# First stage of a two-layer graph network: only the destinations loaded beside x, chunk work moved between the table groups, both zeroings moved behind the first pairs and the first pass

## What is computed

```python
h = jnp.maximum(_layernorm(x), 0.0)
xl, xr = h @ Wl + bl, h @ Wr + br                      # first layer (attention)
m = leaky_relu(xl[src] + xr[dst] + edge_weight1 * We, 0.2)
alpha = softmax of (m @ att) over the edges of one dst
h = gelu(h + segment_sum(alpha * xl[src], dst) + bias)
x = x + batch_norm(h)
h = jnp.maximum(_layernorm(x), 0.0)                    # second layer (messages)
em = relu(layer_norm([h[src], h[dst]] @ msg_w + msg_b)) * edge_weight
messages = mean of em over the edges of one dst
x = x + gate * relu(layer_norm([h, messages] @ upd_w + upd_b)) + (1 - gate) * h
```

## Time and profile before

| | us |
|---|---|
| median of 3 executions | 2472.26 |
| lowest, highest | 2470.81, 2472.52 |
| the profiled execution | 2471.0 |
| its span in the trace | 2469.2 |
| busy: PE, DVE, ACT, POOL | 1646.5, 1522.7, 982.5, 1683.3 |
| first gather, last gather begin | 92.3, 2342.3 |

### The profile page before, as it was taken

How to read it: one execution, slowest core, us unless ns; L and a number is a source line. 1 busy time by engine, 2 the same in 40 slices (tenths; PEclk the granted TensorE clock), 3 DMA queues, 4 the chain that set the end, 5 groups by cost and what they waited for, 6 DMA issues and landing times.

```text
span 2469.2 us, 44266 instructions
## 1 busy us (share of the span) xinstructions
PE 1646.5 (67%) x9934; PEld 1201.4 (49%) x9934; DVE 1522.7 (62%) x4806; ACT 982.5 (40%) x3715; POOL 1683.3 (68%) x1718
## 2 busy tenths in 40 slices
PE   2387778777877777777456666666666666666650
PEld 2255555555555555555344454454454455544550
DVE  5455555555555555555647766666676666667668
ACT  3244334333434343434444444444444344434420
POOL 3377777777777777776017777777777777777732
PEclk9799889898988998999677888888788888889885
DMA  8544344444444344343244444433444444344321
GB/s 257 138 91 86 91 91 87 91 90 90 88 89 91 85 92 89 87 91 72 58 121 98 86 89 92 92 87 89 92 91 86 91 92 92 83 92 93 76 56 52
DMA packets 207823, 228.62 MB, mean 93 GB/s; under 512 B 103103, under 2 KB 153684, under 8 KB 207701
## 3 DMA queue, kind: packets, MB, share of 16 engines
q0 software_dynamic: 54784, 115.94, 24.0%
q1 hardware_dynamic: 152598, 110.34, 16.4%
q10 hardware_dynamic: 384, 1.70, 0.3%
HBM read 194.60 MB, written 33.24 MB: 92 GB/s over the span
## 4 chain that ended last, share of the span: by engine, by line
POOL 56%; issue 19%; PE 8%; DMA 7%; DVE 5%; SPq 1%; ACT 1%; POOLq 1%; ACTq 0%; DVEq 0%
POOL room L667 56%; DMA room<-src_table,rec 5%; PE psum L774 2%; PE psum L704 1%; PE psum L756 1%; PE psum L746 1%; DMA node_x<-in_x 1%; DVE room L1557 1%; PE psum L741 1%; DMA room<-state 1%; DVE stats L1127 1%; PE psum L835 1%; SPq L457 1%; PE psum L764 0%; ACT room L1000 0%
## 5 line engine op out<-in xcount | busy, mean ns | idle before, releaser
L667 POOL DMA_INDIRECT room<-src_table,rec x1664 | 1624.4, 976 | 684.1 <-issue 495.3
L835 PE MATMUL psum<-room,ident 128*128 128x384 f32 (+1 forms) x512 | 292.6, 659 | 377.4 <-DMA room<-src_table,rec 297.9
L1050 ACT ACTIVATE room<-psum 128x128 f32<-128x128 f32 x832 | 218.8, 274 | 585.6 <-DVE room L1478 583.2
L1316 DVE TENSOR_TENSOR room<-psum,room 128x384 f32<-128x384 f32 (+1 forms) x256 | 151.1, 590 | 455.6 <-ACT room L982 367.8
L982 ACT ACTIVATE room<-psum 128x384 f32<-128x384 f32 (+1 forms) x256 | 132.1, 516 | 560.5 <-PE psum L746 557.4
L1478 DVE TENSOR_TENSOR room<-psum,msg_g 128x384 f32<-128x384 f32 (+1 forms) x256 | 151.0, 590 | 315.0 <-PE psum L840 312.8
L746 PE MATMUL psum<-ident,room 128*128 128x128 f32 x832 | 155.4, 305 | 207.4 <-DMA room<-src_table,rec 206.9
L835 PEld LDWEIGHTS psum<-room,ident 128*128 128x128 f32 x512 | 93.1, 227 | 409.7 <-issue 384.7
L853 PE MATMUL psum<-room 128*125 128x128 f32 x1664 | 285.2, 318 | 1.5 <-ACT room L1062 1.5
L774 PE MATMUL psum<-room 128*125 128x128 f32 x1664 | 262.2, 300 | 18.9 <-ACT room L1000 6.3
L840 PEld LDWEIGHTS psum<-room 125*128 125x128 bf16 x2496 | 195.4, 112 | 140.8 <-issue 123.8
(11 more groups left out here) (179 smaller groups left out, 2122.6 us busy)
## 6 DMA issues: line engine op xcount, KB each, us to landing
room<-dst_perm SPq DMA_DIRECT2D x128, 406.2 KB
room<-src_table,rec POOLq DMA_INDIRECT x1664
room<-dst_table SPq DMA_DIRECT2D x128, 62.5 KB
src_table<-room SPq DMA_DIRECT2D x24, 224.0 KB
dst_table<-room SPq DMA_DIRECT2D x24, 224.0 KB
st_in<-state SPq DMA_DIRECT2D x64, 64.0 KB
state<-st_out SPq DMA_DIRECT2D x64, 64.0 KB
st_in<-state SPq DMA_DIRECT2D x64, 62.5 KB
```

What stands on the lines that cost most here:

```text
L667: pool.indirect_dma_start(out=xg[:, u, t * P:(t + 1) * P], out_offset=None, in_=src_table[n][:, :], in_offset=bass.IndirectOffsetOnAxis(ap ...
L835: nc.tensor.matmul(msg_bank[b][:, cols], ident[:, :], xg[:, u, t0 * P:t1 * P], start=True, stop=False, skip_group_check=True)
L1050: i = nc.scalar.activation(sq[:, j * P:(j + 1) * P], msg_bank[b][:, j * P:(j + 1) * P], ACT.Square, accum_out=var_e[:, c, j:j + 1])
```

## The change

Fields: ACT's queue now loads dst alone; src, edge_weight and edge_weight1 are loaded by SP behind the first weights. POOL no longer makes zero_rows or the int16 destinations; ACT makes the latter (`destinations`) between the first norm rows. On ACT the second `deviations` comes in group 2, `weights_part` in groups 3 and 6 (before: ahead of the groups, and 2). On DVE the chunk reductions become `chunk_spans`, before group 2, `rest_of_weights` come before 5 and 8, `count_pairs` before 7, `list_block(0)` before 9, `edge_row_parts` before 10. PE spreads the chunks behind group 5. SP stores the weights behind group 8, the list behind 9, loads dws behind 11, and starts `first_pairs` before the other list blocks; the zeroing of state0 stands behind these, on SP's queue, and `feed` waits for it in slot 2, ahead of the first read of the state. POOL zeroes state1 behind the gathers of the first pass, once the sums of that pass are loaded.

```diff
@@ sync
+            sp.wait_ge(s_padded, 1)
+            for f in (0, 3, 2):
+                load_field(sp, f)
             sp.wait_ge(s_padrow, 3)
             sp.wait_ge(s_edges[0], 48)
...
                 def slot(k, u, end):
                     v = u % 2
+                    if n == 0 and type(k) is int and k == 2:
+
+                        sp.wait_ge(s_zero0, NQ * 16)
...
             for g in range(NG):
                 store_rows(0, g)
-                if g == 5:
+                if g == 8:
                     sp.wait_ge(s_ewp, 4)
...
+                if g == 9:
+                    sp.wait_ge(s_blk3, 1)
+                    sp.dma_start(pair_list[0:P, :], lout).then_inc(s_list, 16)
+                if g == 11:
+                    sp.wait_ge(s_we, 1)
+                    for v in range(2):
+                        sp.dma_start(dws[W:P, v, :, :], we_part[0:P - W, :, :]).then_inc(s_weout, 16)
             sp.wait_ge(s_counts, 1)
             blocks = block_count(sp)
             last = pair_count(sp)
-            sp.wait_ge(s_blk3, 1)
-            sp.dma_start(pair_list[0:P, :], lout).then_inc(s_list, 16)
-            sp.wait_ge(s_we, 1)
-            for v in range(2):
-                sp.dma_start(dws[W:P, v, :, :], we_part[0:P - W, :, :]).then_inc(s_weout, 16)
+            sp.wait_ge(s_rec, 8 * 16)
+            sp.wait_ge(s_ews, 32)
+            sp.wait_ge(s_list, 16)
+            sp.wait_ge(s_pad, 32)
+            first_pairs(0, gat)
             with sp.Fori(1, blocks, 1) as kb:
                 sp.wait_ge(s_blk3, kb + 1)
                 sp.dma_start(pair_list[bass.ds(kb * P, P), :], lout).then_inc(s_list, 16)
-            sp.wait_ge(s_rec, 10 * 16)
+            for q in range(NQ):
+                sp.dma_start(state0[:, :].rearrange("(p t) f -> p t f", p=P)[:, q * QT:(q + 1) * QT, :],
+                             zrow[:, :, :]).then_inc(s_zero0, 16)
             sp.wait_ge(s_list, blocks * 16)
             sp.wait_ge(s_list, 32)
-            sp.wait_ge(s_pad, 32)
-            first_pairs(0, gat)
-            sp.wait_ge(s_zero0, NQ * 16)
             feed(0, gat)
@@ gpsimd
-            pool.memset(zero_rows[:, :, :], 0.0).then_inc(s_zrow1, 1)
-            pool.wait_ge(s_dstf, 1)
-            pool.tensor_copy(dperm[0:n, :].rearrange("c (t p) -> c t p", t=T),
-                             dst_f[0:n, :].rearrange("c (p t) -> c t p", t=T)).then_inc(s_dperm, 1)
...
-            for q in range(NQ):
-                pool.dma_start(state0 ...).then_inc(s_zero0, 16)
-            pool.wait_ge(s_zrow1, 1)
-            settle(pool)
-            for q in range(NQ):
-                pool.dma_start(state1 ...).then_inc(s_zero1, 16)
...
-                pool.wait_ge(s_zero1, NQ * 16)
                 all_pairs(pool, slot, last, 0)

             gather_all(0, gat)
+            pool.wait_ge(s_x[NQ - 1], 64)
+            settle(pool)
+            for q in range(NQ):
+                pool.dma_start(state1[:, :].rearrange("(p t) f -> p t f", p=P)[:, q * QT:(q + 1) * QT, :],
+                               zrow[:, :, 0:D]).then_inc(s_zero1, 16)
             gather_all(1, msg)
@@ tensor
                 project(pe, n, g, weights)
+                if n == 0 and g == 5:
+                    spread_chunks(pe)
@@ scalar
             act.wait_ge(s_padded, 1)
-            for f in (1, 0, 3, 2):
...
+            load_field(act, 1)
...
+            def destinations():
+
+                act.wait_ge(s_dstf, 1)
+                nc.scalar.activation(dperm[0:NCH + 1, :].rearrange("c (t p) -> c t p", t=T),
+                                     dst_f[0:NCH + 1, :].rearrange("c (p t) -> c t p", t=T), ACT.Copy).then_inc(s_dperm, 1)
+
             def tables_of(n):
-                for h in range(2):
-                    deviations(n, h)
+                deviations(n, 0)
                 if n == 1:
+                    deviations(n, 1)
                     act.wait_ge(s_yb, NG)
-                else:
-                    weights_part(0)
                 for g in range(2):
                     norm_rows(n, g)
+                if n == 0:
+                    destinations()
                 for g in range(NG):
+                    if n == 0 and g == 2:
+                        deviations(n, 1)
                     if g + 2 < NG:
                         norm_rows(n, g + 2)
                     features(n, g)
-                    if n == 0 and g == 2:
+                    if n == 0 and g == 3:
+                        weights_part(0)
+                    if n == 0 and g == 6:
                         weights_part(1)
@@ vector
-            tables(0, b_lr, {1: count_pairs, 2: lambda: rest_of_weights(0), 4: lambda: rest_of_weights(1),
-                             6: lambda: list_block(0), 8: edge_row_parts})
+            tables(0, b_lr, {2: chunk_spans, 5: lambda: rest_of_weights(0), 7: count_pairs, 8: lambda: rest_of_weights(1),
+                             9: lambda: list_block(0), 10: edge_row_parts})
...
-            dve.wait_ge(s_rec, 10 * 16)
+            dve.wait_ge(s_rec, 8 * 16)
+            dve.wait_ge(s_ews, 32)
             dve.wait_ge(s_list, blocks * 16)
```

More of the change, by code:

```diff
@@ L177, in gnn_layers @@
         dense = at[0]
-        zero_rows = take(QT * D).rearrange("p (t f) -> p t f", f=D)
         at[0] = U * CH
@@ L225, in gnn_layers @@
         s_padrow = sem("s_padrow")
-        s_zrow1 = sem("s_zrow1")
         s_hrelu = sem("s_hrelu")
@@ L403, in gnn_layers, with load_field @@
         fields = [a["src"], a["dst"], a["edge_weight"], a["edge_weight1"].rearrange("e a -> (e a)")]
+        def load_field(eng, f):
+            to = raw if f < 2 else raw.bitcast(F32)
+            v = fields[f]
+            for c0, c1 in CHUNK_ROWS:
+                eng.dma_start(to[c0:c1, f, :], v[c0 * CH:c1 * CH].rearrange("(c e) -> c e", e=CH)).then_inc(s_edges[f], 16)
+            eng.dma_start(to[FULL_CH:FULL_CH + 1, f, 0:REST_E], row_of(v[FULL_CH * CH:E])).then_inc(s_edges[f], 16)
         first_weights = [
@@ L705, in project, with spread_chunks @@
             i.then_inc(s_proj, 1)
+        def spread_chunks(pe):
+            pe.wait_ge(s_cstat, 1)
+            for q in range(2):
+                i = nc.tensor.matmul(banks[7][:, q * P:q * P + NCH], cstat[0:NCH, q:q + 1].to_broadcast([NCH, P]),
+                                     ident[0:NCH, 0:NCH], start=True, stop=True)
+            i.then_inc(s_crow, 1)
         def tables(pe, n, weights):
@@ L716, in _ @@
             pe.wait_ge(s_ident, 1)
[L717 to L721, removed]
             pe.wait_ge(s_wa, NWA * 16)
@@ L1167, in _ @@
                 layer_norm_scale(0, h)
-            dve.wait_ge(s_dstf, 1)
-            dve.tensor_reduce(cstat[0:NCH, 0:1], dst_f[0:NCH, 0:REST_E], AX_X, ALU.min)
-            dve.tensor_reduce(cspan[0:FULL_CH, 3:4], dst_f[0:FULL_CH, REST_E:CH], AX_X, ALU.min)
-            link(dve.tensor_reduce(cspan[0:NCH, 0:1], dst_f[0:NCH, :], AX_X, ALU.max))
-            link(dve.tensor_tensor(cstat[0:FULL_CH, 0:1], cstat[0:FULL_CH, 0:1], cspan[0:FULL_CH, 3:4], ALU.min))
-            sp_, q_, r_ = (cspan[0:NCH, i:i + 1] for i in range(3))
@@ L1185, in _, with chunk_spans @@
-            link(dve.tensor_tensor(q_, q_, t_, ALU.add))
-            link(dve.tensor_scalar(t_, r_, 0.0, None, ALU.is_lt))
-            link(dve.tensor_tensor(q_, q_, t_, ALU.subtract))
-            dve.tensor_scalar(cstat[0:NCH, 1:2], q_, 1.0, None, ALU.add).then_inc(s_cstat, 1)
+            def chunk_spans():
+                dve.wait_ge(s_dstf, 1)
+                dve.tensor_reduce(cstat[0:NCH, 0:1], dst_f[0:NCH, 0:REST_E], AX_X, ALU.min)
+                dve.tensor_reduce(cspan[0:FULL_CH, 3:4], dst_f[0:FULL_CH, REST_E:CH], AX_X, ALU.min)
+                link(dve.tensor_reduce(cspan[0:NCH, 0:1], dst_f[0:NCH, :], AX_X, ALU.max))
+                link(dve.tensor_tensor(cstat[0:FULL_CH, 0:1], cstat[0:FULL_CH, 0:1], cspan[0:FULL_CH, 3:4], ALU.min))
+                sp_, q_, r_ = (cspan[0:NCH, i:i + 1] for i in range(3))
+                link(dve.tensor_tensor(sp_, sp_, cstat[0:NCH, 0:1], ALU.subtract))
+                link(dve.tensor_scalar(sp_, sp_, 0.0, None, ALU.max))
+                link(dve.tensor_scalar(q_, sp_, 1.0 / W, None, ALU.mult))
+                link(dve.tensor_copy(cint[0:NCH, :], q_))
+                link(dve.tensor_copy(q_, cint[0:NCH, :]))
+                link(dve.scalar_tensor_tensor(out=r_, in0=q_, scalar=-float(W), in1=sp_, op0=ALU.mult, op1=ALU.add))
+                t_ = cspan[0:NCH, 3:4]
+                link(dve.tensor_scalar(t_, r_, float(W), None, ALU.is_ge))
+                link(dve.tensor_tensor(q_, q_, t_, ALU.add))
+                link(dve.tensor_scalar(t_, r_, 0.0, None, ALU.is_lt))
+                link(dve.tensor_tensor(q_, q_, t_, ALU.subtract))
+                dve.tensor_scalar(cstat[0:NCH, 1:2], q_, 1.0, None, ALU.add).then_inc(s_cstat, 1)
```

14 lines of the change are left out of this document (1 added, 13 removed).

## The result

| | before | after |
|---|---|---|
| median of 4 executions, us | 2471.53 | 2455.81 |
| lowest, highest | 2469.22, 2472.52 | 2450.81, 2457.93 |
| the profiled execution | 2471.0 | 2456.3 |
| its span | 2469.2 | 2454.4 |
| first gather begins | 92.31 | 80.54 |

The ratio is 0.9935, with a 95% interval of 0.9918 to 0.9952: faster by more than the 0.2% that can be told. The forecast was 2452.6 and the range 2446 to 2465. The first gather, though, was forecast for 72.6.

What follows compares the result with a forecast made beforehand. POOL's steady gathers were taken to bound the kernel, so only earlier first gathers of a pass could save: 2471.0 - 19.7 (first gather at 72.6 instead of 92.31) + 1.3 (median over profiled execution) = 2452.6 us, range 2446 to 2465.

Steps and rivals of the forecast that it cites:

- rival 1: First stage, SP's queue: weights still take 1.25 us each without zeroes, first gather 82.1, gain 10.2, time 2462.1; chance 0.22.
- What bounds the kernel: Whole kernel: POOL issues a gather every 1.28 us within a pass, so only earlier first gathers of a pass can save.
- part 7: Between the passes: zeroing state1 on POOL takes 2.9 us within 119.94 us of idle POOL, so it costs 0.
- part 6: Start of first pass: zeroing state0 on SP behind the first pairs costs 0, hidden by three pairs of lead; otherwise up to 18 us.
- Part 2: First stage, SP's queue: with the zeroing gone, fifteen weights issue in 0.6 us each, 9 us (bounds 6.6 and 18.8).
- S: First stage: the time SP is free for the tables, forecast 37.5 us (ends 35 and 47), against 43.87 before.
- Part 4: Rest of the tables: 22.4 us of DVE work from row 3, row 12 ends at 64.0, last store issue at 68.0.
- Part 3: First stage, DVE: rows start earlier, row 0 ending at 27 to 30, row 2 by 35 to 39, row 3 starting at 41.6.
- Part 1: Initial loads: x alone with dst arrives at 21 us instead of 27.05 + 1; SP gains nothing there.
- Part 5: End of first stage: 1.0 + 3.6 us from last table store to first gather, at 72.6, 19.7 us earlier.
- Rival 2: Table stage: PE stays at the low clock, groups taking some 4.9 us, first gather at 92, no change, 2471; chance 0.09.
- Rival 4: First stage: the moves do nothing, x not earlier, S 43.9, first gather 79.0, gain 13, 2459; within rival 1's chance.

Runs made afterwards that it cites:

- e5: The control with a spare tensor of state0's size also zeroed on SP's queue, ahead of state0: 2453.74 us, ratio 0.9925 to the kernel before.
- e1: The control with both zeroings back on POOL's queue in the first stage, behind the pads: 2476.95 us, ratio 1.0030 to the kernel before.
- the control: The changed kernel with run-time bounds checks on its two count loads: 2456.21 us, and 2455.12 on another chip; ratios 0.9938 and 0.9943 to the kernel before.
- c0: The control's first run, the changed kernel with run-time bounds checks on two count loads: 2456.21 us, ratio 0.9938 to the kernel before.
- c1: The control run again on a third chip: 2455.12 us, ratio 0.9943 to the kernel before.
- e7: The control with list store, dws loads and later list blocks behind the last table store, ahead of the first pairs: 2458.00 us, ratio 0.9946.
- e3: The control with chunk work, related ACT and DVE work and the weights store back in their old places: 2460.22 us, ratio 0.9962.
- e2: The control with src and both weight fields back on ACT's queue beside x: 2455.31 us, ratio 0.9940 to the kernel before.
- e4: The control with the 15 other weights loaded by POOL's queue instead of SP's: 2449.65 us, ratio 0.9911; repeated on a slow chip, 3232.67 us, ratio 0.9942.
- e8_again: Repeat, at usual pace, of e4's kernel with the ew_perm store and dws loads also on POOL: 2453.60 us, ratio 0.9937 to the kernel before.
- e8: e4's kernel with the ew_perm store and dws loads also on POOL; first run, on a slow chip: 3316 us, ratio 0.9893 to the kernel before.

## Why the prediction was right, and where it was not

The time lies between the forecast (2452.6) and rival 1 (2462.1), nearer to the forecast. The first gather does not: of the signs named for "right", 70 to 75 us for it is the one that failed, and 80.54 is nearer to rival 1's 82.1, though not by rival 1's mechanism. By its steps:

- **What bounds the kernel, part 7, part 6**: right. The first pass takes 1074 us and the second 1056 to 1057, before and after, and the gain comes mainly from the earlier first gather. The stretch between the passes stayed at 119.5, with 4.85 us of zeroing in it (2.9 expected) and its cover intact. The zeroing of state0 costs nothing (e5). The Trainium skill (DMA: Bandwidth & Descriptors, Queues, rings and completion order) has each DMA engine go round its rings by packets and take the descriptors of one ring in order. No row here shows when a single descriptor was served, so that rule stays untested. What shows is when SP issued the record of pair 3, counted from the first gather: 10.7 us before the change (103.05), 18.2 after it (98.69), 23.3 with twice the zeroes (106.49). Three pairs of lead hide that delay.
- **Part 2**: right, and the main one. The 15 weights took 8.5 us, 9 were forecast, and putting the zeroes back costs 13.9 us at the first gather (e1). Its upper bound, 1.25 each, was read from one late load; with the zeroes ahead of all 15 it was 21.0 / 15 = 1.40, and for one of them (bn_gamma) 2.26, where the control took 0.43.
- **S**, the time at which SP is free for the tables: 39.6 instead of 37.5. The records were stored at 31.0, not 28.5: src came at 24.5, not 23, and the stores of rows and dst_perm, costed as short, took 1.87 and 2.28 a pair. Rival 1 (S = 47) did not come: its weights would have had to stay at 1.25.
- **Part 4, the term that was mis-sized**: from the first table store to the last row, 4.1 + 22.4 = 26.5 had been forecast, and it was 72.41 - 39.59 = 32.8. From the end of their issue (41.35) row 0's stores took 4.2 us to land, where the sum had 2.42 from the earlier trace rows: +1.8. They took 4.2 in c0, c1, e5 and e7 as well. The DMAs were no busier than in that row (share 0.68 in 40 to 50 us; 0.82 in 70 to 80 before), so why they took longer stays open. The sum over DVE's work had no term for new waits, and two came: 1.45 for PE (53.68; 3.57 in c0 with its third slow group), and 3.56 before the last row (71.65), as its buffer waits for stores that SP issued behind the ew_perm store, the first of them in 2.54 us instead of 0.8. The sum had charged 2.4 us for such things on SP, but behind the last row, where only the end of the stage shows them. The work between took 0.5 less than summed: together +4.5. S (+2.1), the landing (+1.8) and the waits (+4.5) make 8.4 us; the end of the stage gave 0.5 back (3.2 + 4.93 against 4.0 + 4.6), and 7.9 is the miss of the first gather.
- **Part 3**: the times were right (row 0 at 28.67, row 2 at 37.78, the stall of L1120 gone). What it buys was not asked there: e3 puts the placing at some 4 us.
- **Part 1**: true (x at 20.00, forecast for 21) and worth nothing that shows (e2). The prediction said that all bytes are the same and only their order new, and that SP gains nothing; in fact SP pays for x, with a first record stored at 24.50 where it was 17.18 before and 17.00 in e2.
- **Part 5**: the 4.6 us came out as 4.93. By e7 about half of what the new order of the list gains here is lost between the tables, where part 4 had charged 2.4 us for it.
- **Rival 2** came in part: two groups at 3.75 us, with the clock at 0.50 in 40 to 50 us, and in c0 and e5 a third. The first two lay mostly under DVE's waits and work; the third costs the 2.1 to 2.3 us told at the control. **Rival 4** did not: x was earlier, S too.
- That the time missed by 3.2 us where the first gather missed by 7.9 is luck as much as merit. Some 3.0 us came from pass 2 and the tail, for which the prediction has no step. Over the twelve traces of the usual chips all but the first gather takes 2369.6 to 2376.9 us; the kernel before is at the upper end of it, but so are e4 and e8_again. Whether there is a cause beyond the spread of single traces stays open.

## What to carry to other kernels

A small DMA issue costs what the traffic beside it makes it: 15 loads of weights took 8.5 us of a queue or 21.0, by whether 6.6 MB of zeroes from another engine were under way. Look for bulk traffic that nobody needs yet beside a queue that somebody waits for. And where an engine's lead ends in another queue, as DVE's 16 us did in SP's, both have to move: either half of this change alone brought no earlier first gather. The DMA share did not tell how long a store takes to land (4.2 us at 0.68, 2.42 at 0.82), so give such a term a range, and give the sum a term for waits.

## What was not expected of the hardware

- **Issue under load.** SP's issue of one small load (bn_gamma) went from 0.43 us in the control to 2.26 with POOL's zeroes under way (e1). On SP's own ring five issues of zeroes took 4.17 us, and 7.05 and 7.00 where there were ten (e5); POOL had issued five in 2.86. SP's issue next to the ew_perm store took 2.5 us (2.54 and 2.57), whichever engine had issued that store.
- **Two chips on which the passes took a third longer.** On one the kernel before took 3354 us, on the other 3252, the latter with a mean clock of 0.735 for e4. The first stage took its usual time (first gather at 76.6). In the pass POOL waited where it never waits otherwise; what ended the idle time before the gathers (us, times), first on the slow chip, then for the same kernel on a usual one:

```profile
  DMA rec<-rec_rows: 630.5, 60
  issue: 453.2, 1481
  remote: 196.3, 94
```

```profile
  issue: 497.4, 1632
  DMA rec<-rec_rows: 126.1, 2
```

  The median of one gather was the same, 944 ns. Neither the ratio nor the gain in us carries over with any certainty: e4 gained 19.7 us there and 21.3 on a usual chip, but the kernel of e8 gained 38.3 on its slow chip and 17.1 on a usual one. The cause is open.
